# The four up projections of an MLP in one slot, in a hand-written slot schedule of attention stages

## The reference, cut to what matters

```python
# stage 1 (mlp1): layernorm, up, GELU (tanh form), down, residual
ln_out = layernorm(x, ln3_s, ln3_b)
mlp_out = gelu(ln_out @ w1 + b1) @ w2 + b2
return x + mlp_out
# stage 2 (mlp2): rmsnorm, up, GELU (tanh form), down, residual
out = rmsnorm(attn_out, postnorm_w)
out = jax.nn.gelu(out @ mlp_w1 + mlp_b1) @ mlp_w2 + mlp_b2
return out + residual
```

## Time and profile before

| what | us |
|---|---|
| time, median of 3 runs (lowest to highest) | 2325.23 (2323.97 to 2326.45) |
| profiled execution, its time | 2326.19 |
| profiled execution, its span | 2324.5 |
| PE, ACT, DVE, POOL busy in the span | 2114.0, 1257.4, 1292.8, 680.7 |
| stages 0 to 2, about | 1105 |

### The profile page before, as it was taken

One profiled execution on the slowest core, in us unless ns is written; L12 is line 12 of the kernel. 1 busy time (PEld: TensorE's weight loads), 2 busy tenths in 40 slices (PEclk: granted clock), 3 DMA queues, 4 the chain that ended last, 5 costly groups with the idle time before them and its releaser, 6 DMA issues.

```text
span 2324.5 us, 43553 instructions
## 1 busy us (share of the span) xinstructions
PE 2114.0 (91%) x14880; PEld 1810.9 (78%) x14880; DVE 1292.8 (56%) x4117; ACT 1257.4 (54%) x3924; POOL 680.7 (29%) x618
## 2 busy tenths in 40 slices
PE   4788999999999999897699999999799999999788
PEld 3667777777777777675599999999689999999677
DVE  3658575858576665433455555555545555555654
ACT  2466777786868776644444444444444444444432
POOL 2223333323333333322322222213322221222353
PEclk8899999999999999997799999999999999999989
DMA  6000000000000000000100000000000000000100
GB/s 237 1 4 11 1 10 1 11 1 9 2 2 10 1 4 1 3 1 1 49 24 23 23 18 23 14 23 23 16 24 18 23 14 23 23 23 14 37 14 23
DMA packets 23663, 45.23 MB, mean 19 GB/s; under 512 B 2400, under 2 KB 10080, under 8 KB 22624
## 3 DMA queue, kind: packets, MB, share of 16 engines
q1 hardware_dynamic: 21440, 32.62, 4.5%
q10 hardware_dynamic: 1440, 8.72, 0.9%
q0 software_dynamic: 640, 2.10, 0.3%
HBM read 41.33 MB, written 2.10 MB: 19 GB/s over the span
## 4 chain that ended last, share of the span: by engine, by line
PE 22%; issue 22%; POOL 5%; DVE 2%; ACT 1%; POOLq 0%; ACTq 0%; DVEq 0%
PE general L1573 15%; PE o_psum L1622 2%; PE scores L1610 2%; PE general L1729 2%; POOL probs L1219 1%; POOL w_qk L1195 1%; PE pT_psum L1670 1%; POOL hT L1210 1%; DVE oT L1555 1%; POOL X L1235 1%; POOL w_v L1195 1%; POOL w_o L1195 0%; POOL vrow L1199 0%; DVE oT L1424 0%; ACT oT L1334 0%
## 5 line engine op out<-in xcount | busy, mean ns | idle before, releaser
L430 POOL TENSOR_TENSOR probs<-probs,rsums 128x512 f32<-128x512 f32 (+1 forms) x288 | 283.9, 992 | 670.2 <-DVE rsums L631 669.1
L1219 POOL TENSOR_TENSOR probs<-probs,rsums 128x512 f32<-128x512 f32 x128 | 133.2, 1040 | 764.3 <-DVE rsums L1417 764.3
L470 ACT ACTIVATE probs<-negated,negmax 128x128 f32<-128x128 f32 (+1 forms) x768 | 326.2, 429 | 49.3 <-DVE negmax L622 48.4
L914 PE MATMUL pT_psum<-ident,probs 128*128 128x128 f32 x1088 | 181.8, 290 | 62.1 <-DVE probsT L637 34.4
L1326 ACT COPY probsT<-pT_psum 128x512 f32<-128x512 f32 x128 | 74.9, 585 | 288.8 <-PE pT_psum L1670 288.8
L914 PEld LDWEIGHTS pT_psum<-ident,probs 128*128 128x128 f32 x1088 | 134.0, 148 | 110.6 <-issue 75.2
L1573 PE MATMUL general<-hT,w_qk 128*128 128x512 f32 x768 | 207.0, 405 | 4.2 <-POOL hT L1210 4.2
L1573 PE MATMUL general<-w_o,oT 128*128 128x256 f32 x1536 | 194.6, 281 | 17.0 <-DVE oT L1424 17.0
L1573 PEld LDWEIGHTS general<-w_o,oT 128*128 128x128 f32 x1536 | 186.0, 188 | 25.3 <-DVE oT L1424 18.1
L1573 PE MATMUL general<-ctxT,w_qk 128*128 128x512 f32 x768 | 200.5, 397 | 0.0
L1318 ACT ACTIVATE probs<-scores,negmax 128x128 f32<-128x128 f32 x512 | 180.1, 369 | 29.8 <-DVE negmax L1409 29.7
(11 more groups left out here) (173 smaller groups left out, 4211.2 us busy)
## 6 DMA issues: line engine op xcount, KB each, us to landing
raw_qk<-w_qk_dram SPq DMA_DIRECT2D x34, 256.0 KB, 2.7
raw_v<-w_v_dram SPq DMA_DIRECT2D x17, 256.0 KB, 2.6
raw_vrows<-vrows_dram SPq DMA_DIRECT2D x17, 256.0 KB, 3.2
weights_a<-weights_a_dram ACTq DMA_DIRECT2D x2, 2048.0 KB, 17.7
raw_o<-w_o_dram SPq DMA_DIRECT2D x16, 256.0 KB, 2.6
weights_a<-weights_a_dram ACTq DMA_DIRECT2D x3, 1024.0 KB, 10.0
X<-x_dram SPq DMA_DIRECT2D x8, 256.0 KB, 7.4
ctx_in<-ctx_dram SPq DMA_DIRECT2D x8, 256.0 KB, 4.5
```

The costliest lines, as they stand in the source:

```text
L430: nc.gpsimd.tensor_tensor(pr, pr, rsums[:, n % 4, 0:segs].unsqueeze(2).broadcast_to([P, segs, width(kind) // segs]), ALU.mult).then_inc(s[ ...
L470: last = nc.scalar.activation(probs[:, n % PROBS, i * wide:(i + 1) * wide], src[:, i * wide:(i + 1) * wide], ACT.Exp, scale=1.0 if kind == ...
L914: last = nc.tensor.transpose(pT_psum[:, j * P:(j + 1) * P], probs[:, n % PROBS, j * P:(j + 1) * P], ident[:, :])
L1219: nc.gpsimd.tensor_tensor(pr, pr, rsums[:, t % 2, :].unsqueeze(2).broadcast_to([P, NB, P]), ALU.mult).then_inc(s["probs_ready"], 1)
```

## The change

Only WORK changes. ctx_v goes from slot 37 to 38, mlp2_up0 to up3 all to slot 56, behind ctx_v and ahead of nothing else in it; mlp1_up0 to up3 all to slot 26, behind cross_k. As ctx_v and cross_k are then the first step of their slots, each of the eight up projections is in `work[1:]`: PE issues the four behind each other between the weighing and the odd transposes, and ACT has its eight GELUs behind each other at the slot's end. Slot 1 modulo 18 has no step of WORK left.

```diff
 WORK = [("lat_v", 36), ("ctx_k", 36), ("rms", 54),
-        ("ctx_v", 37), ("mlp2_up0", 55),
-        ("mlp2_up1", 56), ("mlp2_up2", 56),
-        ("cross_o", 21), ("mlp2_up3", 57),
+        ("ctx_v", 38), ("mlp2_up0", 56), ("mlp2_up1", 56), ("mlp2_up2", 56), ("mlp2_up3", 56),
+        ("cross_o", 21),
         ("mlp2_down0", 58),
         ("ln3", 23), ("mlp2_down1", 59),
-        ("chan_q", -12), ("chan_k", -12), ("mlp1_up0", 24),
-        ("self_o", 7), ("chan_v", -11), ("mlp1_up1", 25),
-        ("mlp1_up2", 26), ("cross_k", 8),
-        ("ln2", 9), ("mlp1_up3", 27),
+        ("chan_q", -12), ("chan_k", -12),
+        ("self_o", 7), ("chan_v", -11),
+        ("cross_k", 8), ("mlp1_up0", 26), ("mlp1_up1", 26), ("mlp1_up2", 26), ("mlp1_up3", 26),
+        ("ln2", 9),
         ("cross_q", 10),
```

## The result

| | before | after |
|---|---|---|
| time, median (lowest to highest), 4 runs each | 2324.60 us (2323.24 to 2326.45) | 2297.28 us (2294.00 to 2298.88) |
| profiled execution, its span | 2324.5 us | 2292.3 us |
| ACT's table loads in stages 0 to 2 | 101 | 31 |
| ACT busy in the span | 1257.4 us | 1168.0 us |

The changed kernel takes 0.9880 of the time before (95% interval 0.9863 to 0.9897): 27.3 us less. The prediction was 2308.5 us, 16.7 us less. It named the right direction and the right mechanism and was wrong in size: 2297.28 lies 0.7 us under its range. The two terms that it sized worst are the ends (filling and draining, put at +4 us, measured 9.3) and a low clock behind the new stall (put at -3.4 us, measured 0).

The account below looks back on a forecast made before the run. The prediction took ACT, through its table loads, to bound slots 1 to 4 of each steady period. Gains of 17.5 (mlp2) and 4 (ends) less 3.4 (clock) and 1.4 (mlp1) made 16.7 us: 2308.5 us, range 2298 to 2326.

Parts of the forecast that it names:

- the ends: Filling and draining, with incomplete clusters: a gain of 4 us for both together, bounds -2 and +8.
- a low clock behind the new stall: mlp2's clusters, behind up2's 1.1 us stall: half clock in two of five, costing 3.4 us, bounds 0 and 8.5.
- the five clusters: mlp2's clusters at slots 56, 74, 92, 110, 128: 3.5 us gained in each, 17.5 in all.
- the 0.3 us put behind mlp2_down: mlp2's cluster: ln3 no longer waits, as DVE reaches its norm earlier; 0.3 us gained a cluster.
- mlp1's: Four steady mlp1 clusters, s6 to s9: a loss of 0.35 us each, 1.4 in all; bounds 0 and 3 each.
- The three stalls: PE after the change: 0.25 us in s1, 0.45 in s2 on DVE's copy, 1.1 at up2.
- the 0.5 us to spare that I gave up2: mlp1, s8: ACT reaches its first GELU about 0.5 us before up2 wants the bank.
- A wait on probsT above 1 us in s9: Sign of being wrong: waits on probsT above 1 us in s8 and s9; about 0.6 us was forecast in s9.
- two stalls that would go: First and last mlp1 clusters, in filling and drain: PE's stalls of 2.26 and 2.22 us both go.
- That ACT's time was hidden anyway: Rival, chance 0.13: the ups' waits for the two banks return what the stalls gave; 2322.6 us.
- The slower one: Rival, chance 0.10: in s2 ACT's first GELU comes later, at 4.5 us beyond the layout 2340 us.
- No clock drop at all: Rival, chance 0.17: no half clock, 3.4 us better, 2 us from mlp2_down, ends at +8; 2299 us.

Follow-up runs that it names:

- e7: Changed kernel plus six 128x1 copies on ACT ahead of mlp2's first GELU pair in each group; 2301.14 us, ratio 0.9896 to the kernel before.
- e1: Changed kernel with mlp1's up projections put back as before, so only mlp2's half of the change; 2308.24 us, ratio 0.9929 to the kernel before.
- e2: Changed kernel with mlp2's up projections and ctx_v put back as before, so only mlp1's half; 2323.65 us, ratio 0.9988 to the kernel before.
- e6: Also e6_mixed: changed kernel with mlp1's up projections of groups 2 to 5 spread as before; 2304.73 us, ratio 0.9909 to the kernel before.
- e6_mixed_again: The kernel of e6 run again beside a repeat of the changed kernel; 2308.41 us, ratio 0.9923 to the kernel before.
- e8: Changed kernel with bunching only in steady groups (mlp2 0 to 4, mlp1 2 to 5), old order at both ends; 2302.45 us, ratio 0.9891 to before.
- e5: Changed kernel plus a 128x1 exponential behind each MLP's first three GELU pairs, putting loads back; 2431.70 us, ratio 1.0459 to the kernel before.
- e3: Kernel before with an exponential in place of each GELU, so no table loads in stages 0 to 2; 2274.28 us, ratio 0.9783 to the kernel before.
- after_again: The changed kernel repeated unaltered, beside e6_mixed_again; 2296.40 us, ratio 0.9878 to the kernel before.

## Why the prediction was right in kind and wrong in size

The mechanism held: ACT's table loads paced s1 to s4, and without them mlp2_down comes 3.2 us earlier. What failed are sizes of terms of the sum: +4 us for the ends, measured 9.3; -3.4 us for a low clock behind the stall of up2, measured 0; 17.5 us for the five clusters, measured 19.8, by the 0.3 us put behind mlp2_down; and slot 0, which had no term. One term, mlp1's, erred the other way.

**Loads and ACT's time.** Laid out as 31 loads, 16 and 15, and 89.8 us: measured exactly so, with 89.4 us. (In the last group, slots 152 and 182, no cross_k or ctx_v of a next group stands ahead, so up0 is in `work[:1]` there; no load more comes of it.) The Trainium skill (ScalarE: Activation LUTs, What ACT_TABLE_LOAD costs) adds a drain of about 1380 ns to each load. The traces do not agree: the GELU starts at 574.03, 10 ns after the load that began at 572.74 ended, and no drain is seen.

**mlp2's cluster up to mlp2_down.** This layout held. With the start of s1 set to 562.08, it puts s2 at 565.49 (measured 565.58), up2 at 575.0 (574.93), mlp2_down at 585.14 (585.11). The three stalls were put at 0.25, 0.45 and 1.1 us and measured 0.20, 0.33 and 0.66; of the last, 0.16 us is a slip, as up0 and up1 were laid out at 1.75 us each and not at the 1.83 us of the layout's own rows. 23.03 us against 26.26 are the 3.2 us forecast. The prediction also has its two windows the wrong way round: 26.26 us is the one without a low clock, and 26.20 the one with it, cut just short of the start of mlp2_down at 477.88; both are 26.3 us. Its reading, that the low clock costs little there, stands.

**mlp2's cluster behind mlp2_down.** Here the size was missed. I put 0.3 us there. Four of the five clusters gain 0.6 us behind mlp2_down, 3.8 us in all where I had 3.5, and most of it is ln3's wait on DVE, 0.48 us, which is gone after. Two rows of the kernel before, of the period ahead of that of the earlier trace rows:

```profile
477.88 3.69 PE L803 MATMUL general<-weights_a,upT 128*128 128x256 f32 x16 [0.89 <-ACT upT L528]
...
485.14 0.63 PE L769 MATMUL general<-ident,xhat_y 128*128 128x128 f32 x4 [0.48 <-DVE xhat_y L684]
```

The cluster of the earlier trace rows is the fifth: from mlp2_down to the start of slot 6 it takes 617.22 - 602.90 = 14.32 us, and after the change 598.03 - 585.11 = 12.92: 1.4 us, as mlp2_down ran at half clock in the one (5.20 us) and not in the other (3.72). In five clusters 19.8 us against 17.5: 2.3 us of the miss.

**The granted clock.** I charged 3.4 us for half-clock stretches behind the new stall, in two clusters of five; the choice of two was a guess. There were none in s1 to s5, in any of the profiles of the changed order without added loads, and e7 shows none at a stall of 1.19 us. Another 3.4 us of the miss. The Trainium skill (TensorE: Matmul & The Clock Gate, A second HAM failure mode: psum-queue depth-cycling) has a kernel that cycles through PSUM banks and whose clock oscillates, as PE idles briefly between its groups of matmuls. Here up0 to up3 cycle through two banks with a wait of 0.66 us, and none of the five clusters falls to half clock.

**Slot 0, which I left out.** It has a stall of 2.41 us on DVE, and takes 11.4 us with a half-clock stretch in it and 9.85 without, as the two windows of it after show. Before the change four of five slots 0 were long, after it three of five, 55.2 and 53.9 us together: 1.3 us of the miss. It is no gain that can be counted on, since in e1, e2, e6 and e7 one to five of them are long.

**mlp1's steady clusters.** Forecast at 0.35 us of loss each, measured 0.57. The stall on the odd transposes of s9, put at 0.6 us, is 1.11. PE's timeline:

```profile
613.04 7.17 PE L783 MATMUL general<-hT_y,weights_a 128*128 128x256 f32 x32
...
624.50 0.63 PE L915 MATMUL pT_psum<-ident,probs 128*128 128x128 f32 x4 [1.11 <-ACT probsT L479]
```

All 32 matmuls of the four projections follow each other with no wait, so the 0.5 us to spare that I gave up2 was there. A wait on probsT above 1 us in s9 was one of the signs that I had named for being wrong, and it came: the backlog of ACT behind the four GELU pairs is longer than laid out. 0.9 us the other way.

**The ends.** Put at +4 us between -2 and +8, the largest guess in the sum; measured 4.1 + 5.2 = 9.3, above the bound, and 5.3 us of the miss. The sum named two stalls that would go, 2.26 and 2.22 us. The first one did fall to 0.55 us, but PE now waits for ln2's copy instead, which stands on ACT behind the eight GELUs and the exponentials' load:

```profile
160.43 3.56 PE L783 MATMUL general<-hT_x,weights_a 128*128 128x256 f32 x8 [2.42 <-ACT hT_x L502]
...
164.88 0.41 PE L915 MATMUL pT_psum<-ident,probs 128*128 128x128 f32 x2 [0.55 <-ACT probsT L479]
```

So group 0's cluster gave nothing, and from slot -10 to 36 only 0.7 us are gained. The other 3.5 us of filling are in slots 36 to 54, 111.69 against 108.21 us, where the half-clock stretch at 230.5 of before is missing after. These go with the clock: e6_mixed_again has the new order there and such a stretch, and takes 112.26 us. The three profiles with loads and the old order there (before, e1, e8) all have it, and of six with the new one (the changed kernel twice, e2, e6 twice, e7) one does, so bunching may well have made it rarer; no run shows why. In the drain, slots 132 to 136 gave 2.0 us (24.80 to 22.83), slots 148 to 154 with the second stall 2.6 (31.31 to 28.76), the rest 0.7.

Together: 2.3 + 3.4 + 1.3 - 0.9 + 5.3 = 11.4 us, and 16.7 + 11.4 = 28.1, which is what the traces show without the start. About 5.6 us of it (3.5 in slots 36 to 54, 1.3 in slots 0, 0.8 in one mlp2_down) is half clock that was there before and not after; these runs do not show how much of that the change earned and how much is luck.

**The rivals.** That ACT's time was hidden anyway fell with e1: 16.4 us from mlp2 alone. The slower one needed a first GELU some 2 us or more later, which did not come; that a late ACT stands in PE's way here, e5 shows with 107 us, though by loads and not by late fronts of DVE. "No clock drop at all", 2299 us at a chance of 0.17, is the one that came closest, and it was so for its reason: no half clock in the clusters, and the ends at or above the top of their bounds. My range ended 1 us below it and left no room for the cluster and slot 0 to be mis-sized the same way. e3 shows how far the range might have reached: PE's own work in the cluster is 34.33 us, so 5.4 us a cluster was there to be had, and half-clock stretches before the change amount to 119.5 us in stages 0 to 2 against 78.5 after.

**What stays open.** Where the half-clock stretches fall. The stall of 2.41 us in slot 0 comes with one in some periods and not in others of the same trace, and e6_mixed shows them shifting in stage 3, whose program is the same. So I can say that some of the gain (some 5 us) goes through the clock, but not that the change earned it. Single executions of the kernel before ran from 2319.3 to 2334.6 us, so a difference of a few us between two traces proves little by itself. A GELU computed from functions that share a table with the exponential, if there are such, would take the last 31 loads away and was not tried.

## What to carry to other kernels

Look for stretches where an engine that is half idle over the whole span is busy all the time; if table loads are part of its work there, put the activations of one table behind each other, and reckon the gain as the other engine's stalls in that stretch, not as the loads' time (90 us went, 27 came back). Bunching costs something on its own, 11 us here with no loads in play, and very much if the loads then don't go (107 us), so check in the instruction order that each load really falls away. And when a stage becomes bound by PE, look again at every short stall in it that was covered before; grouped activations also hold up the copies that stand behind them on ACT (2.42 us for ln2's here).

## What the runs showed of the hardware that was not expected

- Where half-clock stretches fall is worth as much as a scheduling change: 12 us between e6_mixed_again and after_again, with 9.3 in a stage that the edit does not touch, against 2.2 us that the edit itself gains in its clusters.
- Single stalls of 0.66 and 1.19 us of PE were never followed by half clock in the clusters. At the stall of 2.41 us in slot 0 a half-clock stretch stands in three periods of five of the changed kernel, in five of e1 and in one of e2.
- A stretch at 1.2 GHz in slot 0 lasts 3.4 us and costs 1.4 to 1.6 us, so nearly half of its length, even though PE has idle time in that slot.
- Where ACT sets the pace, a half-clock stretch of PE can cost nothing: s1 to mlp2_down takes 26.3 us with one in s3 and without one. At mlp2_down, which ACT no longer covers, the same stretch makes the cluster 0.7 to 0.8 us longer (40.5 to 40.6 us in place of 39.8).
